# The row numbers of routing two steps sooner in VectorE's queue, and the block table's operations moved inside the drain

## The reference

```python
def _L0_xattn_ref(q, k, v, w_qs, w_ks, w_vs, w_proj, b_proj):
    qh = jnp.einsum('bld,hdk->hblk', q, w_qs)
    kh = jnp.einsum('bld,hdk->hblk', k, w_ks)
    vh = jnp.einsum('bld,hdk->hblk', v, w_vs)
    attn = jax.nn.softmax(jnp.einsum('hblk,hbmk->hblm', qh, kh), axis=-1)
    out = jnp.einsum('hblm,hbmk->hblk', attn, vh) * qh
    out = out.transpose(1, 2, 0, 3).reshape(q.shape[0], q.shape[1], -1)
    return out @ w_proj.T + b_proj

def _L0_ffn_ref(x, gate_w, w1, w2):
    xt = x.reshape(-1, D)
    logits = jnp.einsum('td,ed->te', xt, gate_w)
    w_topk, sel = jax.lax.top_k(logits, K)          # K = 2
    w_topk = jax.nn.softmax(w_topk.astype(jnp.float32), axis=-1)
    combine = jnp.zeros((T, E)).at[jnp.arange(T)[:, None], sel].add(w_topk)
    h = jax.nn.silu(jnp.einsum('td,edf->tef', xt, w1))
    y = jnp.einsum('tef,efd->ted', h, w2)
    return jnp.einsum('ted,te->td', y, combine)

x = x + tanh(g_xattn[0]) * _L0_xattn_ref(_layernorm(x), ctx, ctx, ...)
x = x + tanh(g_ffn[0]) * _L0_ffn_ref(_layernorm(x), gate_w, w1, w2)
```

## Time and profile before

| | |
|---|---|
| median of 3 runs | 764.19 us (764.18 to 774.77) |
| the profiled execution | 762.03 us, its span 760.3 us |
| TensorE busy, granted clock | 728.7 us, 0.997 of full speed |
| VectorE, ScalarE, GpSimd busy | 584.4, 377.3, 371.3 us |
| attention stage | 0 to about 357 us, its drain from about 340 |
| expert stage | about 357 to 760.3 us |

### The profile page before, as it was taken

The page is one execution under the profiler, slowest core; times in us unless marked ns, Lnnn a source line. Parts: engine busy times, 40 slices in busy tenths (PEclk is TensorE's granted clock), DMA queues, the critical chain, the costliest instruction groups (busy, mean ns, idle before and its releaser), DMA issues.

```text
span 760.3 us, 23505 instructions
## 1 busy us (share of the span) xinstructions
PE 728.7 (96%) x7980; PEld 605.1 (80%) x7981; DVE 584.4 (77%) x1270; ACT 377.3 (50%) x671; POOL 371.3 (49%) x308
## 2 busy tenths in 40 slices
PE   7999999999999999998899999999999999999994
PEld 6567777767677776666789988899999999999994
DVE  5788879798897989796778868767767676767761
ACT  3686676777677667754344422233333333333331
POOL 5135445766676766674424647433343433334332
PEclk9999999999999999999999999999999999999998
DMA  8452443536282725433888875433334333333422
GB/s 302 152 153 98 153 153 131 175 132 216 72 284 77 250 85 197 130 121 111 248 219 215 233 203 103 67 49 48 52 45 55 43 54 48 49 53 45 57 33 26
DMA packets 93177, 93.88 MB, mean 123 GB/s; under 512 B 59312, under 2 KB 77936, under 8 KB 92720
## 3 DMA queue, kind: packets, MB, share of 16 engines
q1 hardware_dynamic: 31184, 64.97, 25.3%
q0 software_dynamic: 13392, 18.03, 13.7%
q10 hardware_dynamic: 48528, 9.92, 7.5%
HBM read 53.89 MB, written 37.95 MB: 121 GB/s over the span
## 4 chain that ended last, share of the span: by engine, by line
PE 39%; DMA 7%; issue 3%; POOL 2%; ACTq 1%; ACT 0%; DVE 0%; POOLq 0%; DVEq 0%
PE h_ps L1483 20%; PE pair_ps L1496 18%; DMA out<-y,meta 7%; POOL records L1742 1%; POOL out L1736 1%; ACTq L158 0%; ACT y L1555 0%; ACTq L160 0%; POOLq L141 0%; PE h_ps L1527 0%; DVE bx_l L1614 0%; POOL last_rstd L1748 0%; ACT bx_h L1543 0%; DVE ht_h L1626 0%; DVE w_now L1620 0%
## 5 line engine op out<-in xcount | busy, mean ns | idle before, releaser
L1736 POOL DMA_INDIRECT out<-y,meta x71 | 132.6, 1868 | 222.5 <-ACT y L1555 191.0
L1483 PE MATMUL h_ps<-bx_h,w_now 128*128 128x128 f16 x2272 | 194.5, 219 | 5.9 <-DVE bx_l L1614 4.5
L1496 PE MATMUL pair_ps<-weights,ht_h 128*128 x1136 | 190.7, 273 | 1.8 <-issue 1.2
L1483 PEld LDWEIGHTS h_ps<-bx_h,w_now 128*128 128x128 f16 x2272 | 152.4, 98 | 11.2 <-DVE bx_l L1614 6.5
L1483 PE MATMUL h_ps<-bx_l,w_now 128*128 128x128 f16 x1136 | 156.2, 219 | 0.5 <-issue 0.5
L1496 PE MATMUL pair_ps<-weights,ht_l 128*128 x568 | 154.8, 273 | 0.0
L1496 PEld LDWEIGHTS pair_ps<-weights,ht_h 128*128 128x128 f16 x1136 | 110.2, 97 | 17.1 <-issue 2.6
L1555 ACT ACTIVATE y<-pair_ps,meta 128x256 f32<-128x256 f32 x71 | 33.7, 474 | 169.3 <-DVE meta L1609 85.2
L1626 DVE CAST ht_h<-hid 128x1024 f16<-128x1024 f32 x71 | 49.7, 700 | 80.9 <-ACT hid L1548 79.7
L1306 POOL TENSOR_TENSOR r_l<-r,r_h 128x512 f16<-128x512 f32 x62 | 75.3, 1214 | 73.7 <-ACT r_h L832 71.8
L1548 ACT ACTIVATE hid<-h_ps 128x1024 f32<-128x1024 f32 x71 | 72.6, 1022 | 63.9 <-PE h_ps L1483 63.1
(11 more groups left out here) (250 smaller groups left out, 1236.5 us busy)
## 6 DMA issues: line engine op xcount, KB each, us to landing
stage<-in_w SPq DMA_DIRECT2D x16, 1024.0 KB
w_split<-split SPq DMA_DIRECT2D x14, 1024.0 KB, 6.5
weights<-w_split SPq DMA_DIRECT2D x14, 1024.0 KB
rows<-records ACTq DMA_DIRECT2D x268, 32.0 KB
xin<-in_x SPq DMA_DIRECT2D x7, 512.0 KB, 5.5
x_even<-in_x SPq DMA_DIRECT2D x4, 512.0 KB
x_odd<-in_x SPq DMA_DIRECT2D x4, 512.0 KB
out<-x_even SPq DMA_DIRECT2D x4, 512.0 KB
```

The source lines that it names most:

```text
L1483: last = nc.tensor.matmul(h_ps[r % 2][:, c, :], w1_now[:, r % 2, s, k * F + c * P:k * F + c * P + P], xt[:, r % 2, k, :], start=(j == 0 an ...
L1496: last = nc.tensor.matmul(y_ps[r % 2], ht[:, r % 2, c, :], weights_at(e, s, WN // 2 + c * D, D).rearrange("p o n -> p (o n)"), start=(c == ...
L1736: pool.indirect_dma_start(out, bass.IndirectOffsetOnAxis(meta[:, r, 0:1].bitcast(U32), 0), y[:, r % 2, :], None, compute_op=ALU.add).then_ ...
```

## The change

The update of the running number gets a function of its own, `count_rows`, and stands in gap 1 of step 5, where `place_rows` was; `place_rows` stands in gap 4 of step 4; `pick_rows` keeps L251 alone. In the drain, the three pieces of the table stand in steps 1, 2 and 3, each directly behind the product with q (`times_q`), and the turning of the rows in step 2 behind them. In the expert stage the two calls follow each other, so the order is the old one.

```diff
-def pick_rows(nc, dve, job_ps, r, s, carry, g):
+def count_rows(nc, dve, job_ps, s, carry, g):
+
     dve.wait_ge(s.route_ops, g * ROUTE + 5)
     nc.vector.tensor_tensor(carry.next_row[:, :], job_ps[:, TG * E:(TG + 1) * E], carry.next_row[:, :], ALU.add).then_inc(s.pos_read, 1)
+
+
+def pick_rows(nc, dve, r, s, g):
+    dve.wait_ge(s.route_ops, g * ROUTE + 5)
     nc.vector.tensor_tensor(r.mask[:, :, :, :], r.pos[:, :, :].unsqueeze(1).broadcast_to([P, 2, TG, E]), r.mask[:, :, :, :],
                             ALU.mult).then_inc(s.route_ops, 1)
...
-            if p == 4 and gap == 1:
-                both_masks(nc, dve, route, routed, g - 2)
+            if p == 4:
+                if gap == 1:
+                    both_masks(nc, dve, route, routed, g - 2)
+                if gap == 4:
+                    place_rows(nc, dve, job_ps, route, routed, carry, g - 2)
             if p == 5:
                 if gap == 1:
-                    place_rows(nc, dve, job_ps, route, routed, carry, g - 2)
+                    count_rows(nc, dve, job_ps, routed, carry, g - 2)
                 if gap == 2:
                     record_weights(nc, dve, route, routed, carry, g - 2, rec[k])
                 if gap == 3:
-                    pick_rows(nc, dve, job_ps, route, routed, carry, g - 2)
+                    pick_rows(nc, dve, route, routed, g - 2)
...
+            if p < 5:
+                times_q(n - 5, NP + p - 5)
+            if p in (1, 2, 3):
+                rest_of_table(p + 3)
             if p == 2:
                 dve.wait_ge(carry.rows_in[0], BLOCK_LOADS)
                 turn_rows(nc, carry.xt, carry.rows, 0).then_inc(carry.x_turned, 1)
-            if p < 5:
-                times_q(n - 5, NP + p - 5)
             if p in (3, 4):
                 dve.wait_ge(r_hi, n - 4)
                 nc.vector.tensor_tensor(r_l[:, (p - 5) % 2, :], r32[:, (p - 5) % 2, :], r_h[:, (p - 5) % 2, :], ALU.subtract).then_inc(last_r_lo, 1)
-            if p == 3:
-                rest_of_table(4)
             if p == 4:
                 dve.wait_ge(carry.x_hi, 1)
                 nc.vector.tensor_tensor(carry.xt_l[:, 0], carry.xt[:, :, :], carry.xt_h[:, 0], ALU.subtract).then_inc(carry.x_lo, 1)
-                rest_of_table(5)
-        rest_of_table(6)
```

More of the change, by code:

```diff
@@ L1681, in routing @@
                 record_weights(nc, dve, route, routed, carry, j, rec[j])
-                pick_rows(nc, dve, job_ps, route, routed, carry, j)
+                count_rows(nc, dve, job_ps, routed, carry, j)
+                pick_rows(nc, dve, route, routed, j)
                 if j == 1:
```

## The result

| | before | changed |
|---|---|---|
| median, 22 runs each | 764.25 us | 760.36 us |
| ratio of the times | | 0.9943, 95% interval 0.9929 to 0.9957 |
| profiled execution, its span | 762.03, 760.3 us | 761.62, 759.9 us |
| first product of the expert stage | 357.32 us | 353.47 us |
| from there to the end of the span | 403.0 us | 406.4 us |

The account below looks back on a forecast made before the run. TensorE was taken to bound the kernel, so only its standstill could be won: 4.7 us in step 5 plus 1.5 in the drain, 6.2 off the median 764.19, giving 758.0 us, range 754.5 to 763.

Parts of the forecast that it names:

- What bounds the kernel: Attention stage: TensorE sets the pace; its wait for the running number in step 5 costs 1.07 us a group, 5.35 in all.
- Sooner update: Step 5, groups 2 to 6: the earlier running number lets TensorE go on 0.94 us sooner a group, 4.7 us in all.
- Is the gain kept?: Steps 5 to 7: TensorE, 0.9 us ahead, next meets VectorE at step 6's second transposes with 0.85 us to spare.
- rival B: Steps 5 to 7: the gap closes but VectorE gives the gain back; 760.3 us with half kept, 762.7 with none; chance 0.13.
- Places: Step 4, six groups with routing: the place operation moves one gap up without a wait, with over 2 us of margin.
- rival C: Steps 5 to 7: TensorE's new phase shifts GpSimd's operations onto VectorE's two-SBUF-input ones; slower, 769.5 us; chance 0.05.
- Drain: End of the attention stage: moved table pieces bring the meeting 1.8 us sooner, less 0.3 for a held piece: 1.5 us.
- Rival A: Drain: VectorE's first table piece waits for two GpSimd operations instead of one, leaving 0.4 us there; 759.1 us; chance 0.17.
- Sum: Whole kernel: 4.7 + 1.5 = 6.2 us gained, giving 758.0 us, with the expert stage only moving along; chance 0.58.
- The signs: Right: step-5 wait gone, meeting 6.2 us sooner. Wrong: new TensorE waits for xt_l, ssub or pn, expert stage not about 403.
- Rival D: Step 5: the running number's update is not what the transposes wait for, so no effect; 764 us; chance 0.03.

Follow-up runs that it names:

- e6: Changed kernel with ScalarE's xn ahead of the exponentials in step 5; 759.51 us against 764.17 for the kernel before.
- e5: Changed kernel with GpSimd's r_l ahead of the indirect row transfer in step 7; 759.59 us against 764.17 for the kernel before.
- e4: Changed kernel with the early table's eighth operation ahead of the places in group 7; 758.22 us against 766.41 for the kernel before.
- e11: The changed kernel unaltered, measured again; 761.21 us against 766.16 for the kernel before, ratio 0.9944.
- e10: Changed kernel with the four edits of e4 to e7 together; 758.31 us against 766.16 for the kernel before, ratio 0.9891.
- e8: Kernel before plus an unused VectorE sum of two SBUF inputs beside GpSimd's pn in step 6; 763.94 us against 764.17 for the kernel before.
- e7: Changed kernel with part 4 of the table behind the drain's last exponent sum; 760.63 us against 764.17 for the kernel before.
- e1: Changed kernel with the drain's loop of the kernel before, so only the row numbers changed; 758.51 us against 766.41 for the kernel before.

## Why the prediction was right or wrong

- **What bounds the kernel** was right: the wait of L547 was the one that cost, it is gone, and all that followed moved with TensorE.
- **Sooner update**, 0.94 a group, measured 0.82. What is late next was named rightly, ScalarE's xn, and its end forecast to 0.02 us (122.06 and 122.08). The transposes follow it by 0.14 instead of the 0.05 taken over from VectorE's release, and the refill saves 0.04 instead of up to 0.10. With xn out of the way (e6) the full 1.06 comes. The five groups give 4.1 instead of 4.7.
- **Is the gain kept?** is the step that failed. It followed TensorE's next input from VectorE, L966, found 0.85 us to spare, and stopped there. It did not follow GpSimd, whose r_l had 0.75 us to spare against a gain of 0.82, behind a chain that starts at VectorE's fixed place. That is 0.87 us of the difference, shown by e5. It is rival B in mechanism, with GpSimd in VectorE's place, at 0.17 of 0.82 and not the half.
- **Places**: "no wait, over 2 us of margin" holds for the places themselves. What was missed is that they push what stands behind them, in one group an operation that had got in ahead of GpSimd by 0.09 us. The prediction used this hold for the drain, and rival C asked for it from TensorE's new phase; it came from VectorE's own new order, which C had taken for unchanged. 0.97 us, once, shown by e4.
- **Drain**: 1.5 forecast, 1.58 measured, by the forecast steps: L1117 held by one operation and not two (1.16 against 1.3), pn late by 0.18 against 0.3, TensorE last at the meeting. Rival A did not come. The hold of L1121 was missed, at no cost.
- **Sum**: 4.7 - 0.6 - 0.87 - 0.97 + 1.5 + 0.08 = 3.84, the measured lead. The expert stage was taken as fixed; its length differs by up to 10 us between profiles, and so the median of many runs is the only time by which the 4 us can be seen. That the time fell within the range owes something to the range, which had been drawn wide enough for nothing of the step-5 gain to be kept.
- **The signs.** The wait of L547 is gone; L665 to L604 of step 5 is 1.16 us, just over the 1.0 to 1.1 named; the meeting comes 3.85 sooner and not 6.2. Of the signs of being wrong, new waits of TensorE did come, but for r_l and x_even, which the list did not have. An expert stage of another length than 403 came too (406.4); the clock's falls, 3.4 us, are as large as the difference, and e11, the same kernel, has none of them, though its stage is long by idle time instead (11.3 us).
- **Rival D** fell with the wait of L547.

## What to carry to other kernels

When a stall of the pacing engine is closed, every producer that used to be early loses as much of its margin: list the spare time of each input of that engine, from every other engine, over the whole period, and compare the smallest with the gain; here it was 0.75 us on GpSimd against 0.82. Moving a small operation also moves what stands behind it in its queue: look for VectorE operations that start within 0.2 us ahead of one of GpSimd's, as an order that differs by 0.1 us can cost a whole GpSimd operation. And a repair moves what stands behind it as well (e10), so it is limited to the place where it was measured.

## What the runs showed of the hardware

- A small VectorE operation with two SBUF inputs that starts beside GpSimd's pn or r_l ends just behind it: 0.55 to 1.08 us for 128x4 elements, and just so with one SBUF input and a constant (0.563 median), whereas a reduction of one SBUF input takes 0.152 in the same place. The form with one input was not expected. The end comes 0.03 us behind GpSimd's for 128x4, 0.08 for 1x64 (L1096) and 0.22 for 1x200 (L1117, L1121).
- One that starts 0.09 us ahead of r_l is not held (L1091 of before, 0.20). To some hundredths the recorded starts do not tell the order: in e10 the table's 1x200 operation starts 0.02 us behind r_l (341.72 and 341.70) and takes 0.30, and r_l pays with 1.34, whereas the last probe of e8 starts with pn and is held.
- GpSimd's indirect transfer holds nothing of this kind: L1091 of the changed kernel, 1x64 with two SBUF inputs, starts at 322.78 within the transfer (322.23, 1.00 us) and takes 0.20.
- GpSimd pays a little too: its r_l takes 1.29 us where it overlaps L1117 of the drain (343.72 in the changed kernel, 344.21 in e7, where L1117 had started ahead of it), and 1.16 in e1, where L1117 stands elsewhere.
- The granted clock can fall to half for some 3.4 us (1.7 us lost) or twice that, after TensorE stood still for 1.5 to 2.8 of the 4 us before, and with more idle time (3.1 us in one wait, e11) it can also stay, in the same kernel.
